# Two of a chunk's three convolution silu blocks moved into the slots of z silus, with the channel blocks grouped otherwise

## What is computed

```python
xn = layernorm(x, ln_g, ln_b) * (1.0 + scale[:, None, :]) + shift[:, None, :]
x_in, z = split(einsum('bsd,ed->bse', xn, in_proj_w), 2)          # 1024 channels each
u = silu(causal depthwise conv of x_in with 4 taps + conv_b)
dt_r, B, C = split(einsum('bsd,ed->bse', u, x_proj_w), [64, 80])   # 16 states
dt = softplus(einsum('bsr,dr->bsd', dt_r, dt_proj_w) + dt_proj_b)
# for every token t, channel d, state n:
#   h = h * exp(dt * A) + dt * u * B ;  y = sum_n h * C
y = (ys + u * D_param) * silu(z)
x = x + gate[:, None, :] * einsum('bsd,ed->bse', y, out_proj_w)
```

## Time and profile before

| | |
|---|---|
| median of 3 runs | 2406.55 us (2406.52 to 2406.91) |
| span of the profiled execution | 2405.4 us |
| PE busy | 2232.3 us, 93% |
| DVE busy | 2163.1 us, 90% |
| POOL busy | 1908.1 us, 79% |
| ACT busy | 1679.7 us, 70% |
| first layer's slot loop | from 68.8 to about 1911 us |

### The profile page before, as it was taken

One profiled execution on the slowest core, in us unless ns is written; L12 is line 12 of the kernel. 1 busy time (PEld: TensorE's weight loads), 2 busy tenths in 40 slices (PEclk: granted clock), 3 DMA queues, 4 the chain that ended last, 5 costly groups with the idle time before them and its releaser, 6 DMA issues. The chain is left out here.

```text
span 2405.4 us, 24262 instructions
## 1 busy us (share of the span) xinstructions
PE 2232.3 (93%) x6966; PEld 1153.2 (48%) x6966; DVE 2163.1 (90%) x2363; ACT 1679.7 (70%) x3268; POOL 1908.1 (79%) x1244
## 2 busy tenths in 40 slices
PE   9899999989998999899989988998987999999999
PEld 3233434334433443344334333433333488988888
DVE  4899999999999999999999999999999966666666
ACT  3688777877787778778877887787555445466655
POOL 0699999999999999999999999999987822232225
PEclk9899999999999999999999999999998999999999
DMA  6610231041104110411051123103100121011113
GB/s 225 229 44 27 100 103 40 27 148 59 35 27 158 47 37 22 167 56 59 19 179 40 31 71 130 33 27 130 64 31 12 74 77 34 26 56 58 49 53 123
DMA packets 78050, 176.10 MB, mean 73 GB/s; under 512 B 7453, under 2 KB 10781, under 8 KB 77918
## 3 DMA queue, kind: packets, MB, share of 16 engines
q1 hardware_dynamic: 77918, 174.56, 21.6%
HBM read 157.23 MB, written 17.30 MB: 73 GB/s over the span
## 5 line engine op out<-in xcount | busy, mean ns | idle before, releaser
L1402 POOL TENSOR_TENSOR arena<-arena 128x1024 f32<-128x1024 f32 x512 | 1199.2, 2360 | 107.1 <-ACT arena L580 77.3
L1001 DVE TENSOR_TENSOR_SCAN arena<-ps,arena 128x512 f32<-128x512 f32 x1024 | 1241.7, 1256 | 1.3 <-ACT ps L580 1.2
L580 ACT ACTIVATE ps<-arena 128x512 f32<-128x512 f32 x1087 | 722.8, 681 | 367.2 <-DVE arena L1001 307.0
L318 PE MATMUL ps<-arena,keep 128*128 128x512 f32 x1782 | 863.3, 615 | 108.2 <-POOL arena L1402 74.9
L989 DVE TENSOR_TENSOR arena<-ps,arena 128x1024 f32<-128x1024 f32 x512 | 618.4, 1208 | 13.8 <-PE ps L318 11.1
L318 PEld LDWEIGHTS ps<-arena,keep 128*128 128x128 f32 x1782 | 333.6, 194 | 592.2 <-issue 338.4
L264 PE MATMUL ps<-arena 128*128 128x512 f32 x1024 | 459.9, 593 | 1.6 <-issue 0.8
L264 PEld LDWEIGHTS ps<-arena 128*128 128x128 f32 x1024 | 193.5, 190 | 248.8 <-issue 247.8
L580 ACT ACTIVATE arena<-arena 128x2 f32<-128x2 f32 (+2 forms) x599 | 228.4, 384 | 52.1 <-POOL arena L1347 17.1
L304 PE MATMUL ps<-arena 128*128 128x512 f32 x512 | 231.1, 592 | 0.0
L1359 POOL TENSOR_TENSOR arena<-arena 128x512 f32<-128x512 f32 x168 | 213.9, 1273 | 10.9 <-ACT arena L580 3.8
(11 more groups left out here) (146 smaller groups left out, 2701.7 us busy)
## 6 DMA issues: line engine op xcount, KB each, us to landing
arena<-scr_bc SPq DMA_DIRECT2D x128, 512.0 KB, 6.4
arena<-in_inT SPq DMA_DIRECT2D x128, 256.0 KB, 2.6
arena<-in_x SPq DMA_DIRECT2D x17, 512.0 KB, 4.3
scr_x<-arena SPq DMA_DIRECT2D x32, 256.0 KB, 2.2
arena_b<-scr_x SPq DMA_DIRECT2D x16, 512.0 KB, 3.8
arena_c<-scr_x SPq DMA_DIRECT2D x32, 256.0 KB, 2.9
out<-arena_c SPq DMA_DIRECT2D x32, 256.0 KB, 2.0
arena<-in_x SPq DMA_DIRECT2D x30, 256.0 KB, 3.3
```

What stands on the lines that cost most here:

```text
L318: last = e.matmul(YP, ident, hb[G % R][:, i, :], start=False, stop=(g == NG - 1 and i == n - 1))
L580: return e.activation(o_, i_, f, **kw)
L1001: e.tensor_tensor_scan(H, DA[s % 4], H, h0, MUL, ADD).then_inc(v_sc)
L1402: m_ = e.tensor_tensor(H, H, Ct[:, GN * g:GN * g + GN, :], MUL)
```

## The change

One table is changed. Keys are slots (j, p) of a chunk, values are the channel blocks from the first up to, but without, the second:

```diff
-        SILU = {(4, 3): (0, 2), (5, 9): (2, 5), (6, 15): (5, 8)}
+        SILU = {(3, 14): (0, 2), (5, 14): (2, 6), (6, 15): (6, 8)}
```

## The result

The changed kernel takes 2416.48 us (median of four runs, 2413.29 to 2418.32), the kernel before beside it 2406.73 (2406.52 to 2408.14): a ratio of 1.0038, with a 95% interval of 1.0023 to 1.0052. It is slower by 9.75 us, and the forecast of 2413.5 named the sign and 7.0 of these. The runs of the changed kernel also spread over 5.0 us where those of before spread over 1.6. The profiled execution has a span of 2414.0 us against 2405.4, so the traces differ by 8.6.

The account below looks back on a forecast made before the run. DVE and, more strictly, POOL bound the kernel. Chunks 0 and 4 lose 1.31 us each, chunk 5 1.26, chunks 1, 2, 6 0.98 each, chunk 3 0.2: 2406.55 + 7.0 = 2413.5 us, forecast 2411.5 to 2416, range 2407 to 2420.

Parts of the forecast that it names:

- What bounds the kernel: In the loop: DVE and POOL both bound it, POOL more strictly, since its delays go through PE into DVE.
- Table loads: On ACT, seven chunks: 28 loads less at 1.283 us, 35.9 us in all, worth nothing by itself.
- the burst at (5, 9): Slot (5, 12): ACT's du_copy already waits 0.72 us for POOL, so removing this burst gains 0.
- The idle of POOL, 1.49 us less 0.18: Behind (5, 14), six chunks: copy 1.91 us later, slack 0.42, POOL idles 1.49; 0.18 is no loss, net 1.31.
- The silu: Burst at (5, 14): the four-block 128x2048 silu would take 1.91 us.
- The gain at (4, 4), 0.33: Burst at (4, 3) removed: POOL's 1.06 us wait goes, but only 0.33 is gained, in chunks 1, 2 and 6.
- Chunk 3, 0.2: No state kept; DVE's scan waits 1.1 us for its exp, mostly taken back: loss 0.2, from 0 to 1.1.
- Chunk 5, 1.26: Net loss of 1.26 us: 1.31 at (5, 14), with 0.05 left of the gain at (4, 3).
- rival 3: (5, 14) to (7, 2): TensorE's clock drops, about 1.75 us each, one in each of four chunks: 2420.5; chance 0.12.
- Rivals 1 and 2: 1: fewer bursts clear y_fin's waits at (4, 6), 2398.5, chance 0.09; 2: POOL's idle absorbed, 2406.5 to 2411, chance 0.19.

Follow-up runs that it names:

- The copy ahead of the burst: Changed kernel with the 128x2 copy of pair (5, 12) issued ahead of the silu burst in slot (5, 14): 2408.64 us, ratio 1.0006.
- the late copy: Kernel before, with only the copy of pair (5, 12) made later, in slot (6, 0): 2411.89 us, ratio 1.0019.
- the first half alone: Kernel before, with only the two silu blocks of (4, 3) moved to (3, 14): 2406.48 us, ratio 0.9995.
- the other half: Kernel before, with (4, 3) kept and four silu blocks at (5, 14): 2417.72 us, ratio 1.0043.
- the filler in chunk 0: Changed kernel with four matmuls of zeros on PE in unit 6 of chunk 0: 2419.57 us, ratio 1.0046.
- the early projection: Kernel before, with only the projection of block 2 moved from slot (4, 2) to (4, 0), with evacuation and taps: 2411.65 us, ratio 1.0021.
- the fastest version: Kernel before, with silu blocks of (4, 3) moved to (3, 14) and block 2's projection moved to slot (4, 0): 2403.95 us, ratio 0.9986.
- the second trace: Trace from running the changed kernel a second time, unedited: 2417.19 us, ratio 1.0042.

## Why the prediction held, and where it didn't

**What bounds the kernel: right.** It called POOL the stricter bound and DVE the one whose own delays are made up. The copy ahead of the burst and the late copy show both halves: 8.0 us of DVE's waits, with POOL's rest of 0.46 per chunk, cost 1.4 us, or 2.2 against the run with the first half alone, and 5 us of POOL's alone cost 4.7. It isn't without exception: in chunk 5, with little waiting for PE left, DVE gave back only 0.3 of 1.1 us.

**Table loads and the burst at (5, 9), worth 0: right.** ACT's wait of 0.72 became 2.49, so its saved time is idle time. The trace has 28 loads less of 1.283 us, 35.9 us, with the next instruction 0.01 to 0.02 us behind a load, and the kernel is slower. Against this stands the advice of the Trainium skill, page "ScalarE: Activation LUTs", section "Rules for kernel authors", to group by table set; here the measurement decides.

**The idle of POOL, 1.49 us less 0.18: slightly too large.** It is 1.39 to 1.42 in six chunks. The silu was right (1.912), but its duration isn't what it adds to ACT's chain: it starts at 479.30, while the z silus ahead of it run to 478.33 + 1.09 = 479.42 by the timeline. From `du_copy` to the copy it is 483.15 - 475.10 = 8.05 us, against 478.79 - 472.54 = 6.25 before: 1.80 more, not 1.91. That is the difference of 0.1 in POOL's wait. A net of 1.2 us would have been nearer. What made the hole is the order and not the silu's length alone: with the small copy ahead of the same 1.91 us of silu, 0.46 is left.

**The gain at (4, 4), 0.33: right.** 0.3 to 0.4 us in each of chunks 1, 2 and 6 with that half alone, and 0.2 to 0.3 between the other half and the whole. The wait of 1.06 went, and what remains are two smaller ones, for the copy and for the taps:

```profile
423.88 9.29 POOL L1402 TENSOR_TENSOR arena<-arena 128x1024 f32<-128x1024 f32 x4 [0.18 <-ACT arena L580]
433.69 2.69 POOL L1359 TENSOR_TENSOR arena<-arena 128x512 f32<-128x512 f32 x2 [0.52 <-ACT arena L580]
```

**Chunk 3, 0.2: near.** It lost 0.4. DVE's wait there was nearly the forecast 1.1, and two thirds were given back. In the other six chunks this wait is 0.6 to 1.2 us, where about 1.2 was named for all:

```profile
943.91 1.28 DVE L1001 TENSOR_TENSOR_SCAN arena<-ps,arena 128x512 f32<-128x512 f32 x1 [1.02 <-ACT ps L580]
```

**Chunk 5, 1.26: right.** It lost 1.2 us: POOL's wait of 1.39 less the 0.18 it waited before. With the late copy it is 0.85 less 0.18, and the chunk loses 0.6. That the copy ahead of the burst doesn't help this chunk is no argument against it: there a drop of the clock at its start and DVE's own wait make up the same sum. That chunk 7, whose instructions are the same, differs by 0.5 between traces stays open; over all kernels it lies between 229.1 and 230.3.

**The drop of the clock, rival 3: the term that was missing.** The mechanism, the stretch ((5, 14) to (7, 2)) and the size were named: 1.75 us each was the price given, and 1.9 to 2.2 were measured (chunk 0: 3.5 - 1.31; chunk 6: 232.4 - 230.5; chunk 1 with the filler in chunk 0: 232.4 - 230.4). Two steps failed. The argument against it, that PE has a backlog of three sums there, holds behind slot (5, 14) but not ahead of the projection at (6, 14), where PE has none and waits 1.90 us. And it was held against the forecast, with 0.12, as if one excluded the other, and with four drops in every execution. Also missing is that a drop may cost nothing when it ends within PE's waits for POOL. The measured time is the forecast with one or two drops added: 2413.5 + 2.1 = 2415.6 or 2417.7, where the medians are 2416.5 and 2417.2.

**Rivals 1 and 2: out.** `y_fin` still waits 8.4 us, so it wasn't the bursts that held it up; and the periods did grow in spite of what DVE gets back. (The 7.9 us of rival 1 are eight waits, of which the six at (4, 6) make 6.8; that changes nothing.)

## What to carry to other kernels

A loaded share tells which engine has time in hand, not which of its instructions are waited for. Before lengthening or merging work on a half-idle engine, look for the small instruction behind it that releases a buffer or feeds the engine that is nearly full, and read its slack in the timeline: here a slack of 0.42 us, overrun by 1.4, outweighed 28 saved table loads, and moving one 0.19 us copy ahead of the burst gave nearly all of it back. Then test edits in pairs where one clears the way for the other: the early projection lost 5.2 us alone and, with the burst moved away, made the fastest version.

## What the runs showed of the hardware

TensorE's granted clock fell ahead of the projection where PE had idled only a little more than before: 1.90 us instead of 1.76 in chunk 0, and 0.74 at line 314 instead of none. In all traces without fillers it fell in 14 of 35 such places with a wait of 1.88 us or more for POOL, and in none of 41 with 1.76 or less. Both traces of the changed kernel have the drop in chunk 0, and both have one in chunk 6, where only that of the second trace cost time. What it took, in extra time of the records of chunk 0, is 0.63 + 1.80 + 0.47 = 2.9 us, so some 6 us ran at 1.2 GHz. With the copy ahead of the burst line 314 waits 0.87 us in chunk 0, but the wait for POOL is 1.17, and there is no drop. Whether a given chunk has one differs between executions of the same program, and what decides it was not found. Drops elsewhere in the loop come in every kernel, that before included; the one at the start of chunk 5 with the copy ahead of the burst made an expand wait 1.46 us. Eight records of zeros, 0.47 us each, kept the drop away ahead of all seven projections in the one execution traced, and ahead of the one in the run with fillers in chunk 0 alone. That they work through PE's activity, and not by shifting the sums a little, was not separated, nor was it shown that all of the spread of the runs (2413.3 to 2418.5 over nine runs of the changed kernel) comes from these drops.
